# A ViT tower's output written by tiles of two images, in four transfers, with the class tokens issued by GpSimd

## The reference, cut to what matters

```python
h = _L0_tok_ref(x, L0_tok_w, L0_tok_b)
h = jnp.concatenate([jnp.broadcast_to(cls_tok, (h.shape[0], 1, h.shape[2])), h], axis=1)
h = h + _L0_attn_ref(_layernorm(h, axis=-1), ...)
h = h + _L0_ffn_ref(_layernorm(h, axis=-1), ...)
h = h + _L1_attn_ref(_layernorm(h, axis=-1), ...)
h = h + _L1_ffn_ref(_layernorm(h, axis=-1), ...)
return h
```

## Time and profile before

| | us |
|---|---|
| median of 3 runs (331.24 to 332.14) | 331.63 |
| the profiled execution's own time | 332.05 |
| its span, first to last instruction | 329.9 |
| PE busy | 290.9 |
| DVE busy | 263.9 |
| ACT busy | 211.1 |
| POOL busy | 13.7 |

### The profile page before, as it was taken

One profiled execution on the slowest core, in us unless ns is written; L12 is line 12 of the kernel. 1 busy time (PEld: TensorE's weight loads), 2 busy tenths in 40 slices (PEclk: granted clock), 3 DMA queues, 4 the chain that ended last, 5 costly groups with the idle time before them and its releaser, 6 DMA issues.

```text
span 329.9 us, 6328 instructions
## 1 busy us (share of the span) xinstructions
PE 290.9 (88%) x2375; PEld 264.4 (80%) x2375; DVE 263.9 (80%) x782; ACT 211.1 (64%) x519; POOL 13.7 (4%) x38
## 2 busy tenths in 40 slices
PE   8989999999999999999979126199797999999994
PEld 6979769999999999999958014178575599999993
DVE  0347778999998989998877899889859779999962
ACT  1055477777686667777658398787051788888860
POOL 0340000000000000000010002300000000000000
PEclk9999999999999999999999555589969999999999
DMA  7990403503150504020000000002300026433402
GB/s 238 284 315 25 169 3 93 207 0 150 52 200 2 201 0 170 5 108 0 2 1 3 0 0 2 0 0 87 138 2 0 2 72 209 147 124 126 118 3 50
DMA packets 10542, 27.29 MB, mean 83 GB/s; under 512 B 1352, under 2 KB 2184, under 8 KB 10512
## 3 DMA queue, kind: packets, MB, share of 16 engines
q1 hardware_dynamic: 9776, 26.01, 23.8%
q0 software_dynamic: 416, 0.68, 0.7%
q10 hardware_dynamic: 320, 0.20, 0.3%
HBM read 26.43 MB, written 0.45 MB: 81 GB/s over the span
## 4 chain that ended last, share of the span: by engine, by line
DVE 40%; PE 33%; ACT 16%; issue 5%; DMA 3%; SPq 2%; DVEq 0%; ACTq 0%
PE bank L648 11%; ACT hid_hi L1114 7%; DVE hid_lo L1474 7%; PE bank L628 5%; DVE hidden_area L1469 5%; DVE fc_lo L1448 4%; DVE pj_parts L1451 4%; PE bank L717 4%; DMA score_area<-w_l_dram 3%; ACT pj_parts L1092 3%; PE bank L618 3%; PE bank L700 2%; PE bank L698 2%; PE bank L678 1%; DVE score_area L1761 1%
## 5 line engine op out<-in xcount | busy, mean ns | idle before, releaser
L1114 ACT ACTIVATE hid_hi<-hidden_area 128x260 fp32r<-128x260 f32 x144 | 56.3, 422 | 33.5 <-DVE hidden_area L1469 31.3
L648 PE MATMUL bank<-hid_hi,pj_parts 128*128 128x260 f32 x288 | 76.3, 286 | 0.1
L1474 DVE TENSOR_TENSOR hid_lo<-hidden_area,hid_hi 128x260 fp32r<-128x260 f32 x144 | 57.0, 427 | 9.7 <-ACT hid_hi L1114 0.6
L648 PEld LDWEIGHTS bank<-hid_hi,pj_parts 128*128 128x128 f32 x288 | 54.1, 188 | 1.1 <-DVE hid_lo L1474 0.5
L1107 ACT ACTIVATE hidden_area<-bank 128x260 f32<-128x260 f32 x144 | 49.0, 377 | 6.4 <-PE bank L700 5.6
L618 PE MATMUL bank<-zeros 128*128 128x260 bf16 x239 | 34.8, 300 | 8.3 <-ACT hidden_area L1259 6.4
L648 PE MATMUL bank<-xt_hi,fc_hi 128*128 128x260 f32 x144 | 41.2, 286 | 0.3
L700 PE MATMUL bank<-xt_lo,fc_lo 128*128 128x260 f32 x144 | 41.4, 288 | 0.0
L717 PE MATMUL bank<-hid_hi,pj_parts 128*128 128x260 f32 x144 | 40.7, 283 | 0.0
L648 PE MATMUL bank<-hid_lo,pj_parts 128*128 128x260 f32 x144 | 40.7, 282 | 0.0
L648 PE MATMUL bank<-xt_lo,fc_hi 128*128 128x260 f32 x144 | 40.7, 282 | 0.0
(11 more groups left out here) (297 smaller groups left out, 557.1 us busy)
## 6 DMA issues: line engine op xcount, KB each, us to landing
raw_area<-fc_dram SPq DMA_DIRECT2D x8, 768.0 KB, 4.4
raw_area<-pj_dram SPq DMA_DIRECT2D x8, 576.0 KB, 5.6
xn<-comb_dram SPq DMA_DIRECT2D x12, 260.0 KB, 3.8
raw_area<-fc_dram SPq DMA_DIRECT2D x6, 512.0 KB, 4.1
embed_area<-embed_in_dram SPq DMA_DIRECT2D x8, 352.0 KB, 6.7
hidden_area<-comb_dram SPq DMA_DIRECT2D x9, 260.0 KB, 4.0
raw_area<-pj_dram SPq DMA_DIRECT2D x6, 384.0 KB, 4.4
score_area<-w_l_dram SPq DMA_DIRECT2D x1, 576.0 KB, 10.4
```

The source lines that it names most:

```text
L648: mm = pe.matmul(out, lhs[a], rhs[b], start=start and n == 0, stop=stop and n == 2, skip_group_check=True)
L1114: act.activation(hid_hi[:, x % 3, tok], hid_w[:, x % 2, tok], ACT.Copy).then_inc(hid_hi_ready[y], 1)
L1474: dve.tensor_tensor(hid_lo[:, x % 3, tok], hid_w[:, x % 2, tok], hid_hi[:, x % 3, tok].bitcast(F32), ALU.subtract).then_inc(hid_lo_ready[y ...
```

## The change

The patch tokens go out by tiles of `h`, two images a transfer, so in four transfers: SP issues tiles 0 and 2, ScalarE tiles 1 and 3. The class tokens' transfer moves from SP to GpSimd, behind all of GpSimd's other work, and has a semaphore of its own, for which SP waits at the end too. Nothing else is changed.

```diff
+        out_done_pool = sem("out_done_pool")
...
-        def patches_out(queue, b, done):
-
-            lo = (b % 2) * PATCH
-            queue.dma_start(t["out"][b, 1:S, :], h[lo:lo + PATCH, b // 2, :]).then_inc(done, 16)
+        def patches_out(queue, i, done):
+
+            queue.dma_start(t["out"][2 * i:2 * i + 2, 1:S, :], h[:, i, :]).then_inc(done, 16)
...
-            for b in (0, 1, 4, 5):
-                sp.wait_ge(h_done, 4 + b // 4)
-                patches_out(sp, b, out_done)
-            sp.wait_ge(h_done, 6)
-            sp.dma_start(t["out"][:, 0, :], h[0:B, 4, :]).then_inc(out_done, 16)
-            sp.wait_ge(out_done, 16 * 5)
-            sp.wait_ge(out_done_act, 16 * 4)
+            for i in (0, 2):
+                sp.wait_ge(h_done, 4 + i // 2)
+                patches_out(sp, i, out_done)
+            sp.wait_ge(out_done, 16 * 2)
+            sp.wait_ge(out_done_pool, 16)
+            sp.wait_ge(out_done_act, 16 * 2)
...
+            pool.wait_ge(h_done, 6)
+            pool.dma_start(t["out"][:, 0, :], h[0:B, 4, :]).then_inc(out_done_pool, 16)
...
-            for b in (2, 3, 6, 7):
-                act.wait_ge(h_done, 4 + b // 4)
-                patches_out(act, b, out_done_act)
+            for i in (1, 3):
+                act.wait_ge(h_done, 4 + i // 2)
+                patches_out(act, i, out_done_act)
```

## The result

| | us |
|---|---|
| before, median (6 runs, 330.32 to 332.14) | 331.27 |
| changed, median (6 runs, 336.66 to 338.88) | 337.62 |
| ratio, with its 95% interval | 1.0197 (1.0169 to 1.0225) |
| forecast, with its range | 339.6 (336.3 to 343.8) |
| the changed kernel's profiled execution | 337.11, its span 335.2 |

The changed kernel is 6.5 us slower (331.27 x 0.0197). The runs of one kernel spread over some 2 us, so for all that follows a second measure is read from each profile: the **output stretch**, from SP's first output issue to the end of the span. It was 329.9 - 324.89 = 5.0 us before and is 335.2 - 323.18 = 12.0 us now. In this execution the first issue came 1.7 us earlier than in the one shown of before; 1.4 of them were there already when SP issued the first reload of weights (30.96 against 32.34), long before anything that the change touches.

The account below looks back on a forecast made before the run. The end was taken as bound by output issues, after the change by two shared DMA engines: data from 326.1 plus 11.0 us plus 0.83 gives 337.9 against 329.9, +8.0 on 331.63 = 339.6 us, range 336.3 to 343.8.

Parts of the forecast that it names:

- What bounds the end: After the last sums no compute engine works; the last 4.0 us are output, bound by issues, not by bytes.
- Part 1: Output issues: four instead of eight; with data spread as before they would end 1.4 us earlier, at most.
- rival C: Output over 16 engines, GpSimd landing like SP after 2.4 us: -1.1 us, 330.5 us; chance 0.06.
- Part 2: Output transfers: destination's outermost count of 2 allows only 2 DMA engines, 256 rows on each.
- The same two engines for all four transfers: Output from SP and ACT: all four transfers fall on the same two engines, 256 rows each in one line.
- Price of a row: Output rows on two engines: 43 ns each, so 256 rows take 11.0 us; 30 to 60 ns considered.
- Part 3: Class tokens from GpSimd: landing at 328.3 to 331.9, under the patch transfers' data until 337.1, so 0.
- the 0.4 us that GpSimd was to be later: Class tokens at the end: by the skill's first-byte latencies they would land some 0.4 us later than from SP.
- Rival B: Output over 16 engines, GpSimd's class tokens last, landing after 6.0 us: +2.5 us, 334.1 us; chance 0.06.
- Its limit of 3.5 us: Class tokens' landing: GpSimd decides the end once it takes over 3.5 us, 329.4 - 325.9.
- A: Output transfers use two engines each, but SP's are others than ACT's: +2.8 us, 334.4 us; chance 0.08.

Follow-up runs that it names:

- counts 4 and 8: Changed kernel, class tokens by SP, each 128-row transfer cut over 4 or 8 images of the output: stretch 6.8 and 4.7 us, ratios 1.0085 and 0.9991 to before.
- single images on ACT: Changed kernel with ACT's transfers by single images, SP's by pairs, class tokens by SP: stretch 7.7 us, ratio 1.0094 to before.
- one queue: Changed kernel with all four pair transfers and the class tokens issued by SP: stretch 11.3 us, ratio 1.0195 to before.
- the last kernel: Changed kernel with each transfer taking two images of one side of the partitions from neighbouring tiles, class tokens by GpSimd: stretch 4.5 us, ratio 0.9981 to before.
- the kernel with two images of one side: Four transfers, each two images of one side from neighbouring tiles; class tokens by SP 4.3 us stretch, ratio 0.9971; by GpSimd 4.5 us, 0.9981.

## Why the prediction was right

- **What bounds the end** (no compute after the sums, only the output can move): right. The adds to `h` and the first issue stand as before; all 7.0 us lie behind them.
- **Part 1, fewer issues.** The mechanism is right and its size somewhat too large. Where the issues are fewer and the engines stay 16, the stretch fell by 0.7 us; 1.4 were forecast at most, and 1.1 in rival C.
- **Part 2, over how many engines.** Right, and it is the whole loss: 2 completions a transfer were forecast, 2 were found, and 260 packets on ACT's queue. The rows of before showed that the outermost count sets the number of engines, but not which side's count; that the smaller decides was an argument and a rule then, and the runs with counts 4 and 8, where only the destination's count differs, show it for these shapes. The same two engines for all four transfers: right, shown by the runs with single images on ACT and with one queue.
- **Price of a row.** This is the term that was mis-sized. I took 43 ns: 256 rows took 10.0 us in the DMA view above, 39 ns, and in the steady part 5.5 us at 47 GB/s, 33 ns. So in the steady part two engines work as fast as the fastest rows of before, and the second queue on them costs nothing. The 33 ns alone would give 8.4 us; some 1.5 us are lost in the first 3 us of data, which run at 23 to 27 GB/s. That start was in no row of before. With 39 instead of 43 ns the sum is +7.0 us, which is the stretch's: its other two terms, 1.2 us from the first issue to the first data and 0.83 from the last data to the end, are 1.2 and 0.8 in the changed kernel. That 43 ns came so near is partly luck, since 39 is the mean of a slow start and a faster rest, and the working had no such start. Of the 2.0 us between 339.6 and 337.62 the row's price makes 1.0 and the median of before, 331.27 over six runs in place of 331.63 over three, 0.4; the rest lies within the spread of the runs.
- **Part 3, GpSimd.** The term of 0 was right, and little cover was needed: where the line is gone, GpSimd in place of SP made the stretch 0.2 us longer (5.0 to 5.2, 4.3 to 4.5), which the runs don't resolve. Its upper end of 6.0 us to landing, from loads at the kernel's start, said nothing of the end of the kernel, where an idle GpSimd takes 1.8 to 2.5 us; that the changed kernel's 5.9 us lie so near it is luck. No profile has a time to landing for the same transfer from SP, so the 0.4 us that GpSimd was to be later stay unmeasured. Rival B had this price wrong: with 16 engines the change would not have been slower. Its limit of 3.5 us, too, is where GpSimd would make the kernel slower than before; with the data over at 327.7, GpSimd would have been the last to land from about 2 us on, as C's own sum with 2.4 us shows.
- **Rivals.** A fell by two runs. B and C fell by the count of completions. What C described, four transfers over 16 engines with a quick GpSimd, is the last kernel, and it comes out at 0.9981 of before, in place of C's 0.9966 (330.5 against 331.63).

What stays open is the start of the line. With GpSimd the first 2.1 us of data ran at 27 GB/s, without it at 26, and with all transfers on SP at 31, always below the 47 of later. In the changed kernel the first 1.0 us (324.4 to 325.4) has 43 rows of SP's queue and none of ACT's, at 33 GB/s. So neither GpSimd nor the second queue is its cause alone, and no run shows what is.

## What to carry to other kernels

In these runs a transfer from SP or ACT was as fast as the number of engines that its outermost dimension could be cut over, on the side where that count is smaller. Before merging transfers, look at the outermost count of both access patterns, and count the small packets per transfer in the profile, which say how many engines took part. If merging brings a small dimension to the front (images, heads, batches), put the partitions first by merging along another dimension instead; the same number of transfers then keeps all the engines. Fewer issues are worth little (0.7 us here for four fewer), and the wrong cut cost ten times that.

## What the runs showed of the hardware that I had not expected

- One DMA engine moved about 23 GB/s of 768 B rows to DRAM with two, four or eight engines at work (47, 94 and 182 GB/s). With 16 engines and transfers of 64 rows the whole output of before ran at 121 GB/s; in short stretches of the kernel with two images of one side 16 engines reached 335 to 363.
- The same transfer from GpSimd landed in 1.8, 2.5 or 5.9 us, and between these kernels only the transfers of the other queues differ. A time to landing is not a property of the issuer alone.
- Eight engines with 64 rows each (4.7 us) are as good as 16 engines with single images (5.0 us), and they do it with four issues fewer. Before the change the 16 engines were busy for only 51.2% of the time, so there was room.
- An issue can itself take long. With all four pairs on SP, the class tokens' issue took 2.02 us, where it took 0.49 before; one of the four pairs' issues took 2.50 us and the shortest 0.55. The line on the two engines was long by then, but no run shows that it is the cause.

```profile
329.04 2.02 SPq L552 DMA_DIRECT2D out_dram<-h  x1
```
